# Four 32-row matmuls side by side for the spreading of the heads, and one dense matmul of zeros ahead of each set of row maxima and of linear scores

## The reference, cut to what matters

```
Q = _split_heads(x @ WQ.T, h)            # h = 16 heads of 8 channels
K = _split_heads(x @ WK.T, h)
scores = einsum('bhqd,bhkd->bhqk', Q, K) / sqrt(8)
scores = where(causal, scores, NEG)
m = max(scores, -1, keepdims=True)       # the row maxima
e = exp(scores - m)
attn = e / sum(e, -1, keepdims=True)
```

## Time and profile before

| | |
|---|---|
| runs | 3520.96, 3529.91, 3533.36 us; median 3529.91 |
| profiled execution | 3520.73 us, its span 3518.9 us |
| TensorE clock granted, mean | 0.799 of full |
| TensorE busy | 2765.0 us, 79% |
| TensorE weight loads | 1622.9 us |
| VectorE busy | 1817.1 us, 52% |
| ScalarE busy | 1881.9 us, 53% |
| GpSimd busy | 3.6 us |

### The profile page before, as it was taken

How to read it: one execution, slowest core, us unless ns; L and a number is a source line. 1 busy time by engine, 2 the same in 40 slices (tenths; PEclk the granted TensorE clock), 3 DMA queues, 4 the chain that set the end, 5 groups by cost and what they waited for, 6 DMA issues and landing times.

```text
span 3518.9 us, 46207 instructions
## 1 busy us (share of the span) xinstructions
PE 2765.0 (79%) x18736; PEld 1622.9 (46%) x18736; DVE 1817.1 (52%) x2770; ACT 1881.9 (53%) x1764; POOL 3.6 (0%) x12
## 2 busy tenths in 40 slices
PE   7999898767987789877898678986789867897215
PEld 4766456343563445634456344553445534454102
DVE  5464655535555455554555445554465544664434
ACT  3433235764357633576335763457534575336994
POOL 0000000000000000000000000000000000000000
PEclk9997989668896688966889668886689866888557
DMA  3000000000000000000000000000000000000000
GB/s 129 1 1 1 19 1 1 1 1 7 1 1 1 1 7 1 1 1 1 7 1 1 1 1 7 1 1 1 1 4 1 1 1 1 4 1 1 0 0 6
DMA packets 4560, 19.38 MB, mean 6 GB/s; under 512 B 609, under 2 KB 865, under 8 KB 3809
## 3 DMA queue, kind: packets, MB, share of 16 engines
q1 hardware_dynamic: 4320, 16.10, 1.2%
HBM read 14.00 MB, written 2.10 MB: 5 GB/s over the span
## 4 chain that ended last, share of the span: by engine, by line
PE 54%; ACT 20%; DVE 14%; issue 12%; DMA 0%; DVEq 0%; ACTq 0%; SPq 0%
ACT back_cosines L1318 7%; PE one_ps L1707 3%; ACT back_cosines L1320 3%; PE two_ps L683 3%; PE one_ps L860 2%; PE two_ps L1273 2%; PE one_ps L683 2%; PE two_ps L555 2%; DVE back_nsum L1328 2%; PE one_ps L835 2%; PE two_ps L908 2%; PE one_ps L841 2%; PE two_ps L999 1%; ACT front_scratch L931 1%; PE two_ps L860 1%
## 5 line engine op out<-in xcount | busy, mean ns | idle before, releaser
L1318 ACT ACTIVATE back_cosines<-back_cosines 128x4096 f32<-128x4096 f32 x128 | 458.0, 3610 | 0.5
L931 ACT ACTIVATE front_scratch<-one_ps 128x1152 f32<-128x1152 f32 x168 | 171.7, 1022 | 267.5 <-PE one_ps L846 267.3
L1328 DVE TENSOR_REDUCE back_nsum<-back_cosines 128x8 f32<-128x2048 f32 x64 | 143.1, 2279 | 246.5 <-ACT back_cosines L1318 246.5
L1320 ACT ACTIVATE back_cosines<-back_cosines,wts 128x4096 f32<-128x4096 f32 x64 | 236.6, 3700 | 5.0 <-DVE back_cosines L1391 4.7
L795 DVE TENSOR_REDUCE front_negm<-one_ps 128x8 f32<-128x1024 f32 (+1 forms) x168 | 203.7, 1220 | 41.0 <-PE one_ps L770 40.0
L835 PE MATMUL one_ps<-ident_bf,mask_q 128*128 128x256 bf16 x480 | 95.1, 307 | 91.4 <-ACT front_scratch L931 79.4
L1707 PE MATMUL one_ps<-front_xn,wts 128*128 128x512 f32 x252 | 139.8, 683 | 31.4 <-DVE front_scratch L1738 31.4
L1273 PE MATMUL two_ps<-back_cosines,back_vs 128*18 128x256 f32 x896 | 91.9, 559 | 70.1 <-DVE back_vs L1340 70.1
L1391 DVE TENSOR_SCALAR back_cosines<-two_ps 128x2048 f32<-128x2048 f32 x56 | 128.3, 2290 | 32.3 <-PE two_ps L1255 32.2
L694 ACT ACTIVATE back_cosines<-two_ps,wts 128x512 fp32r<-128x512 f32 x28 | 19.3, 688 | 230.1 <-PE two_ps L908 230.1
L764 PE MATMUL one_ps<-front_qkr 32*128 32x128 f32 (+1 forms) x896 | 127.3, 390 | 17.9 <-issue 10.3
(11 more groups left out here) (624 smaller groups left out, 6151.4 us busy)
## 6 DMA issues: line engine op xcount, KB each, us to landing
wts<-w_dram SPq DMA_DIRECT2D x1, 4184.0 KB, 18.0
front_xin<-x_dram SPq DMA_DIRECT2D x8, 256.0 KB, 4.4
out_dram<-back_z SPq DMA_DIRECT2D x8, 256.0 KB, 2.0
wts<-w_dram SPq DMA_DIRECT2D x1, 1903.0 KB, 7.1
wts<-w_dram SPq DMA_DIRECT2D x1, 1736.5 KB, 21.8
wts<-w_dram SPq DMA_DIRECT2D x1, 1152.0 KB, 16.6
wts<-w_dram SPq DMA_DIRECT2D x3, 256.0 KB, 8.5
wts<-w_dram SPq DMA_DIRECT2D x1, 516.5 KB, 4.9
```

Of the source, the lines that this page charges most:

```text
L931: nc.scalar.activation(h.probs[:, e % 2, 0:n * HEADW].rearrange("p (k c) -> p k c", c=HEADW), h.ps[:, 0:n, 0:HEADW], ACT.Exp, scale=float( ...
L1318: nc.scalar.activation(cosines, cosines, func, scale=scale).then_inc(h.arc_pass.sem, 1)
L1320: nc.scalar.activation(cosines, cosines, func, scale=scale, bias=C(bias)).then_inc(h.arc_pass.sem, 1)
L1328: nc.vector.tensor_reduce(h.nsum[:, kt, :].rearrange("p (g2 j) -> p j g2", g2=2), h.cosines[:, u % 2, kt * 4 * TOK:(kt + 1) * 4 * TOK].rea ...
```

## The change

It has five parts.

1. The selection matrices of the spread become one 128x128 matrix for each table instead of four; the columns of the q and k weights (and the biases in arccos) are permuted when the weights are packed, so that the four heads of tile g lie in rows 32g to 32g+31. A spread is then 8 matmuls with 32 rows of contraction and 128 columns of weights, still 512 columns moved, the first four (`_of_high`) into banks 0 to 3 from row blocks 0 to 3, then the other four (`_of_low`). The order is by table first and by tile second; the semaphore steps come after the sixth and the eighth matmul.
2. `dense_pe` issues `clear_ps` over one bank, once at the head of each set of row maxima and of each set of linear scores (`DENSE`): 12 in each of three causal stages and 12 in the linear stage of a pass, 48 in a pass, 384 in all. The bank is one that the set then overwrites. The other places have a count of 0.
3. A constant `own` replaces `blk8` in `linear_state_dve`, for the permuted heads.
4. The block of constants is 1408 columns narrower (3 x 128 x 4 fewer, 128 more), and four of the six selection tables that VectorE rounds at the start (L1977) have 128 columns instead of 512.
5. The run lengths for "fronts" and "backs" of all three engines are others; those of "both" are unchanged.

```diff
-              ("den", HPG * P), ("dense", HPG * P), *((n, GROUPS * P) for n in SPLITS),
+              ("den", HPG * P), ("dense", HPG * P), *((n, P) for n in SPLITS), ("own", P),
+DENSE = {"max": 1, "linear": 1, "scores": 0, "arccos": 0, "mqa_max": 0, "mqa": 0}
...
-            for g in range(GROUPS):
-                for i, table in enumerate(tables):
-                    last = nc.tensor.matmul(h.ps[:, g, :], picks[table][:, g * P:(g + 1) * P], halves_of(h, first + i),
-                                            start=(i == 0), stop=(i == 1))
-                if g % 2:
-                    last.then_inc(done.sem, 1)
+            for i, table in enumerate(tables):
+                for g in range(GROUPS):
+                    last = nc.tensor.matmul(h.ps[:, g, :], picks[table][rows(g, QUAD), :], halves_of(h, first + i)[rows(g, QUAD), :],
+                                            start=(i == 0), stop=(i == 1), skip_group_check=True)
+                    if i == 1 and g % 2:
+                        last.then_inc(done.sem, 1)
...
+        def dense_pe(h, bank, site):
+            for _ in range(DENSE[site]):
+                clear_ps(h.ps[:, bank, :])
...
                 elif m >= 2:
                     pe.wait_ge(h.max_done.sem, h.max_done.at(turn, s, m - 1))
+                dense_pe(h, js.start, "max")
...
                         pe.wait_ge(h.k_ready.sem, h.k_ready.at(turn, s, 2))
+                    dense_pe(h, 0, "linear")
...
-            own = C("blk8").unsqueeze(1).broadcast_to([P, PAIR, P]).rearrange("p b (h d) -> p b h d", d=HD)
+            own = C("own").unsqueeze(1).broadcast_to([P, PAIR, P]).rearrange("p b (h d) -> p b h d", d=HD)
...
-            splits[n][p, head % GROUPS, QUAD * (head // GROUPS) + HD * i + dim] = float(mine)
+            splits[n][p, QUAD * (head % HPG) + HD * i + dim] = float(mine)
...
+    grouped = np.arange(P).reshape(HPG, GROUPS, HD).transpose(1, 0, 2).ravel()
-        return {"q": q, "k": k, "v": v, "o": o}
+        return {"q": q[:, grouped], "k": k[:, grouped], "v": v, "o": o}
```

More of the change, by code:

```diff
@@ L492, in build @@
             first = cols["const"][2][n][0] - skip
-            picks[n] = nc.alloc_sbuf_tensor_at(f"picks_{n}", [P, HPG * P], F32R, offset=wts_base + 4 * first)
+            picks[n] = nc.alloc_sbuf_tensor_at(f"picks_{n}", [P, cols["const"][2][n][1]], F32R, offset=wts_base + 4 * first)
         weff = sb("weff", [P, 6 * P])
@@ L832, in causal_scores_pe @@
                         pe.wait_ge(h.probs_ready.sem, h.probs_ready.at(turn, s, e))
+                    dense_pe(h, 0, "scores")
                     for k in range(len(heads)):
@@ L1121, in mqa_pe @@
                         pe.wait_ge(h.max_done.sem, h.max_done.at(turn, s, 2 * m - 1 + j // 2))
+                    if j % 2 == 0:
+                        dense_pe(h, j, "mqa_max")
                     last = nc.tensor.matmul(h.ps[:, j, 0:SEQ], h.q4[rows(j, MQD), 0, m * P:(m + 1) * P],
@@ L1141, in mqa_pe @@
                     qs = slice(b * SEQ, (b + 1) * SEQ)
+                    dense_pe(h, 0, "mqa")
                     for kt in range(2):
@@ L1251, in arccos_pe @@
                         pe.wait_ge(h.part_ready.sem, h.part_ready.at(turn, s, u - 1))
+                    dense_pe(h, 0, "arccos")
                     for g2 in range(2):
@@ L1996, in _constants @@
         dense[QUAD * (head // HPG) + first + dim, head % HPG, p] = 1.0
-    splits = {n: np.zeros((P, GROUPS, P), np.float32) for n in SPLITS}
+    splits = {n: np.zeros((P, P), np.float32) for n in SPLITS}
     for i in range(QUAD // HD):
         for n, mine in (("q_of_high", i < 2), ("q_of_low", i >= 2), ("k_of_high", i % 2 == 0), ("k_of_low", i % 2 == 1)):
-            splits[n][p, head % GROUPS, QUAD * (head // GROUPS) + HD * i + dim] = float(mine)
+            splits[n][p, QUAD * (head % HPG) + HD * i + dim] = float(mine)
     later = (p[None, :] > p[:, None])
@@ L2023, in _constants @@
             "half": col(0.5), "one": col(1.0), "ln1024": col(np.log(1024.0)), "lin_eps": col(LIN_EPS), "den": den.reshape(P, -1), "dense": dense.reshape(P, -1),
-            **{n: t.reshape(P, -1) for n, t in splits.items()}}
+            "own": (GROUPS * (head[:, None] % HPG) + head[:, None] // HPG == head[None, :]).astype(np.float32), **splits}
 def _rows(v):
@@ L2073 @@
                 "down": _chunks(a["L2_ffn_down_w"].T[None])},
-        "arccos": {"q": qkv3[:, 0:P], "k": qkv3[:, P:2 * P], "v": qkv3[:, 2 * P:], "o": a["L3_attn_w_out"].T,
-                   "bq": b3[0:P, None], "bk": b3[P:2 * P, None], "bv": _rows(b3[2 * P:]), "bo": a["L3_attn_b_out"][:, None]},
+        "arccos": {**headed(qkv3[:, 0:P], qkv3[:, P:2 * P], qkv3[:, 2 * P:], a["L3_attn_w_out"].T),
+                   "bq": b3[0:P][grouped, None], "bk": b3[P:2 * P][grouped, None], "bv": _rows(b3[2 * P:]), "bo": a["L3_attn_b_out"][:, None]},
         "qlora": {"bias": a["L3_ffn_biases"].T, "gamma": a["L3_ffn_ln_gamma"].T, "beta": a["L3_ffn_ln_beta"].T},
```

## The result

| | before | after |
|---|---|---|
| median of 20 runs each | 3527.66 us | 3493.99 us |
| lowest and highest | 3513.63, 3540.49 | 3467.16, 3527.16 |
| ratio | | 0.9903 [0.9877, 0.9929] |
| profiled execution, its span | 3520.73, 3518.9 | 3469.77, 3468.0 |
| prologue (to the first linear score) | 426.1 | 432.3 |

The change brings 34 us; I forecast 128 under the first three runs (3392 us), in a range of 3340 to 3500. An iteration is 10 us shorter (forecast 18), and prologue and epilogue together are 8 us longer, where 33 us less was forecast. The runs of the changed kernel also lie 60 us apart, those of the kernel before 27 us, and its profiled execution is at the low end. Median and extremes are of all 20 runs; the ratio leaves out the four runs of the changed kernel that lie in the slow state (3519.3 to 3527.2 us), and with them the ratio of the means is 0.9920.

The account below looks back on a forecast made before the run. No engine was full; TensorE held 54% of the chain of waits, slowed by half clock behind the head. From 3520.73 us, less 81, 47 and 3, it came to 3390, or 3399 by the median; forecast 3392 us, range 3340 to 3500.

Parts of the forecast that it names:

- Part 1, the spreads: All spreads: about 0.71 us each, saving 60 us in six iterations, 6 in the prologue, 15 in the epilogue; 81 us.
- Rival D: Spreads: the row blocks wait for each other, so the spreads gain 0; 3471 us, chance 0.05.
- Part 2, the dense matmuls: Sets of maxima and linear scores: dense matmuls keep TensorE's clock up; 57 us, less 10 for some passes, 47 us gained.
- The clock holds at 1 through this stretch: Linear scores and causal0's maxima: dense matmuls keep full clock in most passes; 10 us gained an iteration there.
- VectorE hides them, just: Pairs of linear set and maxima at full clock: TensorE needs 2.14 us with dense matmuls, VectorE 2.17 us.
- rival A: Head's pairs: waits between VectorE and TensorE replace the slow clock, dense matmuls gain 0; 3437 us, chance 0.19.
- Prologue and epilogue: Dense matmuls outside the iterations: 9 us gained, about one head's, most of it in the epilogue.
- Rival B: Head: clock falls at the shortened spreads and stays at 0.5, dense matmuls cost 0.43 us each; 3502 us, chance 0.13.
- allowance of 10 us: Dense matmuls: taken off for one pass in five where the clock is already at half when a stretch begins.
- Parts 3 to 5: Constants up to 2 us earlier, fewer roundings 1 us, taken as 3 us; run lengths 0, give or take 10 us.
- Rival C: Full stretches such as 474 to 618 us fall to half clock; slower, 3598 us, chance 0.06.
- marks against the forecast: Wrong if an iteration exceeds 430 us, the head's clock is 0.5 with dense matmuls, or L743 waits over a us.

Follow-up runs that it names:

- experiment 4: The changed kernel with no dense matmuls and with the run lengths of the kernel before: 3471.09 us, ratio 0.9866.
- experiment 2: The kernel before with only the dense matmuls added, spreads and order as before: 3531.81 us, ratio 1.0022.
- 6: The changed kernel with dense matmuls only in the linear sets and causal0's maxima, none in causal1 and causal2: 3452.68 us, ratio 0.9792.
- 10: The changed kernel with dense matmuls only in causal0's maxima and at the head of each spread of linear and causal0: 3436.10 us, ratio 0.9761.
- Experiment 11: The changed kernel with dense matmuls in the linear sets, causal0's and causal2's maxima and the spreads of linear and causal0: 3463.87 us, ratio 0.9831.
- experiment 1: The changed kernel with no dense matmuls, new spreads and new run lengths kept: 3456.38 us, ratio 0.9810.
- experiment 3: The changed kernel, dense matmuls included, with the run lengths of the kernel before: 3511.90 us, ratio 0.9953.
- 9: The changed kernel with dense matmuls only in the linear sets, causal0's maxima and the spreads of linear and causal0: 3442.66 us, ratio 0.9763.
- 5: The changed kernel with dense matmuls in the linear sets alone, none in the sets of maxima: 3508.13 us, ratio 0.9938.

## Why the prediction was right or wrong

**Part 1, the spreads: the price and the overlap right, the sum of 81 us too large.** 0.74 us a spread (0.71 taken from L1122), busy sum 67 us (60 forecast), and VectorE's copies late next, as the timeline shows. The places in the profiled iteration: head 2.5 us (3.0), causal2 2.2 (2.7), arccos 2.2 (2.8), causal1 1.5 (1.5); 8.4 of 10.0 us. As a part done alone it makes 0.9810, 67 us of 3528, with the run lengths in it, and 0.9866, 47 us [34, 61], without them; forecast 81. In the profile of experiment 4 the six iterations give 52 us of the forecast 60 and the prologue 6 of 6 (419.8 us), but the epilogue, forecast 15 us shorter, is 2 us longer (474.0). So the epilogue is the piece that failed, for which I had no row of its spreads. With the new run lengths it is 14 us shorter (458.6), so what it gains hangs on the order of its steps; why stays open. The early clock falls of two of the iterations take some of the rest. Rival D is out. The Trainium skill ("TensorEngine Tiling (Array Packing)", PSUM Bottleneck) says that the copy out of PSUM may become the next limit; copies of 1.22 us against a spread of 0.74 agree.

**Part 2, the dense matmuls: this step failed, the term of 47 us.** Its effect was a loss: adding them to the spreads takes 0.9810 to 0.9903, and 0.9866 to 0.9953 with the old run lengths, 33 and 31 us of 3528, both clear of their intervals. On the old spreads they lose 8 us (experiment 2). By its own steps:
- "The clock holds at 1 through this stretch": in the profiled iterations it holds for 29 to 31 us behind the first score where it held for 10 to 12. Mostly right there.
- "VectorE hides them, just": wrong. The pair was sized right (2.22 against 2.14 us), but VectorE needs 8.34 us of the first 10, so it isn't what TensorE can hide behind. The forecast took VectorE's work, 30 us, for the length of the twelve pairs. The work is 29.6 us (24.93 and 4.68 in 859 to 896), but the pairs take 35.9 us (859.12 to 895.01), before 38.1. In the chain from 858.81 to 887.08 us, three groups of linear sets, 21 dense matmuls stand with 5.65 us in all, 0.27 each, and the last group runs at half clock. The 6 us behind the pairs became 4.7 and not 3 (the prediction's own step from 6 to 3 is 3 us, where it writes 2.5). The head gained 2.4 us and not 10.5. This is rival A's picture, the pairs nearly as slow as they were; its 3437 us would still have needed dense matmuls that cost nothing elsewhere.
- causal2: forecast a cost of 2 us, measured 3.0: its twelve reductions take 17.6 us from the first start to the last, and 14.6 in 45 of the 48 profiled iterations without dense matmuls there; in the other three (16.1 to 18.2 us, one each before, in 6 and in 10) the clock falls within this stretch, as in none of the 30 with them. 12 x 0.27 = 3.2. Experiment 11 agrees: 21 us in all, 2.6 in each of the eight passes.
- causal1: forecast 0, and the iterations agree: from causal1's first spread to the next head 242.0 us in the quickest, with its dense matmuls (the changed kernel) and without (experiments 1 and 6).
- Prologue and epilogue: forecast 9 us of gain. With dense matmuls the prologue is longer in all three pairs: 9.7 us (432.3 against 422.6), 16.0 with the old run lengths (3 against 4), 12.6 on the old spreads (2 against before). Prologues with the same work differ by up to 9 us, so the sign is sure and the size isn't. The epilogue is 15.3, 2.3 and 0 us longer, so what it pays isn't settled. Here I carried over a gain from the head to stages that I had no row of.

**Rival B: right in mechanism, wrong in how it strikes.** I gave it 0.13, as a case of the whole execution. It strikes single heads: iterations of 449 us against 427 in experiment 3, of 446 in 6. In the profile of the changed kernel no iteration is struck, but the head of the epilogue is: there the clock falls 0.3 us behind the first score, for 27 us, with TensorE busy 26.09 of 27 and dense matmuls in the sets.

```profile
2994.00:3021.00 27.00, 26.09 (x201) 14.40 (x201) 15.21 (x20) 2.90 (x5) 0.00 (x0) 0.51 0.00 1
```

That profile is 51 us under that of the kernel before, the medians 34; iterations of this kind in its other runs would make the difference and the spread of 60 us. The recorded clocks of the 20 runs fit: the mean granted clock goes from 0.813 in the quickest (3467.16 us) to 0.793 in the slowest (3527.16 us), 30 us for each 0.01. A slow iteration of experiment 3 takes 22 us more with 48 us more at half clock, 0.007 of the mean clock, so 32 us for each 0.01; about three of them make the 60 us. It remains an argument, since none of the longer of these runs was profiled. The allowance of 10 us for such passes was taken off without knowing that they cost 22 us each.

The Trainium skill ("TensorE: Matmul & The Clock Gate", Why this matters for your kernels) ties the lower clock to gaps in the matmuls. Here the measurement decides otherwise: at 864 to 900 us of experiment 3 TensorE is busy 35.94 of 36 us, and the clock is 0.51. Nor does the prediction's own reading, that the share of the array in use goes with the clock, settle it: the good head of experiment 3 has the same matmuls and stays at 1.00.

**Parts 3 to 5.** The block of constants lands in 5.5 us and not 7.1, 1.6 us of the 3 forecast. The run lengths, taken as 0 and up to 10 either way, brought 15 to 20 (experiments 3 and 4). So by experiments the terms are 47 for the spreads (81 forecast), a loss of 31 to 33 for the dense matmuls (gain of 47), 15 to 20 for the run lengths (0): together 29 to 36 us, where 34 were measured.

**Rival C** didn't come: an iteration's mean clock is 0.81 (0.79 before), though short of the mark of 0.85. Of the marks against the forecast, an iteration over 430 us isn't met in the profile, and L742 waits 0.28 us; a clock of 0.5 with the dense matmuls in the stretch is met in the epilogue's head and in two iterations of experiment 3. The mark of 419 us is missed by 8.

**The sum again**, in profiled executions: forecast 108 us in six iterations and 33 outside, less 10; measured 59 and -8. So the iterations miss by 49 us and the rest by 41, against which stand the 10 taken off: 80. The head's pairs alone would make the 49 (6 x 8.1), but the other places miss too: the spreads' 8.4 us and the head's 2.4 less causal2's 3.0 are 7.8 of the 9.8 us gained. The other 2 lie between causal1's first spread and the next head, 246 us before and 242 to 244 after; this stretch takes 242.0 to 246.7 us within experiment 1 alone, so no part can claim them. Outside, the dense matmuls are 25 us by experiment 1, 18 and 12 by the other two pairs.

Open: where exactly prologue and epilogue pay, since the prologues of 9, 10 and 11, which do the same work, differ by up to 9 us (432.1, 425.6, 423.3); what decides in which heads the early fall comes; whether any full-width matmul in front of the spreads would do, or only a delay; and why 12 dense matmuls in the linear sets alone (5) are the worst choice, while the 12 in causal0's maxima with the spreads (10) do as well as all of them (9). 5 has no dense matmul in the spreads, so these two differ in more than the place, and no run has causal0's alone.

## What to carry to other kernels

A filler matmul that keeps the clock up is worth its time only where the clock would fall without it and its cost stays under what it gives: count it on the chain at full price, and don't let another engine's busy time "hide" it unless that engine is the bound in every us of the stretch, its own waits included. Place fillers set by set and measure each place; twelve a pass in causal0 are in both of the quickest versions, the same twelve in causal2 cost 21 us. Fillers also make a bad case worse: with the clock at half an early fall cost 22 us with them and 5 without. When a change makes a dense piece of work short, look at what runs behind it at what clock, in several iterations and not in one.

## What the runs showed of the hardware

- TensorE's clock is 0.50 or 0.51 with the engine busy 88%, mostly with matmuls of 32 rows or 18 columns, and 99.8% (experiment 3), there with 18 dense matmuls among them; and with dense matmuls of zeros in every set it holds 1.00 for 29 us (changed kernel) where it fell after 10.
- The same instructions in the same order run at 1.00 for 29 us in one iteration and at half clock for 58 us in another (experiment 3).
- Four row blocks side by side: eight matmuls of 32 rows and 512 columns took 0.74 us, at full rows 2.04 to 2.12. Accumulating in each bank from two tables doesn't stand in the way.
- A dense matmul of 512 bf16 columns costs 0.22 us on the chain behind one of 128 rows, 0.32 behind one of 18 columns, 0.56 at half clock.
- The 20 runs of the changed kernel lie 60 us apart, with mean clocks of 0.793 to 0.813; the five with one more matmul in each spread 9 us, with 0.816 to 0.821.
